# Sampling by matmuls with row weights in place of indirect gathers, in a chain of four convolution layers

## The reference, cut to what matters

```
x = x + L0(_gn(x))   # patches of 8x8 in 10x10 windows: one of 8 experts per patch (argmax of the
                     # routing logits), 3x3 convolution, bias, relu, times the softmax probability
x = x + L1(_gn(x))   # 3x3 convolution with weights mixed from 4 experts per image
x = x + L2(_gn(x))   # every pixel replaced by its nearest of 512 codes of 32 channels
x = x + L3(_gn(x))   # 3x3 deformable convolution:
    px, py = positions of 9 taps per pixel, from a 1x1 convolution of the input
    sampled = bilinear sample of the image at (px, py), zero outside
    out = 3x3 convolution, stride 3, of the sampled taps
```

## Time and profile before

| | us |
|---|---|
| median of 3 runs | 3292.12 (3291.43 to 3294.28) |
| the profiled execution | 3283.97 |
| its span, first to last instruction | 3282.1 |
| POOL busy | 2332.2 |
| PE busy | 1852.2 |
| DVE busy | 1597.8 |
| ACT busy | 710.1 |
| mean granted clock of PE, share of full | 0.711 |

### The profile page before, as it was taken

One profiled execution on the slowest core, in us unless ns is written; L12 is line 12 of the kernel. 1 busy time (PEld: TensorE's weight loads), 2 busy tenths in 40 slices (PEclk: granted clock), 3 DMA queues, 4 the chain that ended last, 5 costly groups with the idle time before them and its releaser, 6 DMA issues.

```text
span 3282.1 us, 31069 instructions
## 1 busy us (share of the span) xinstructions
PE 1852.2 (56%) x10418; PEld 1066.7 (33%) x10418; DVE 1597.8 (49%) x2862; ACT 710.1 (22%) x1865; POOL 2332.2 (71%) x2324
## 2 busy tenths in 40 slices
PE   5666775286743866367752966347862767422222
PEld 3343433153422533144331534124431534201000
DVE  3383476334753367334763357434673347522222
ACT  1141232022311323122320223112320223100000
POOL 1007777777777777777777777777777777777776
PEclk9887886588755977578765987569865788555555
DMA  4005213332135213152134222252132421211111
GB/s 81 20 25 116 69 52 89 78 76 71 52 91 106 70 51 89 54 103 69 52 90 98 64 65 69 73 104 69 52 88 57 99 70 52 83 52 54 53 52 48
DMA packets 225793, 230.24 MB, mean 70 GB/s; under 512 B 147028, under 2 KB 184324, under 8 KB 224612
## 3 DMA queue, kind: packets, MB, share of 16 engines
q0 software_dynamic: 74352, 152.18, 17.1%
q1 hardware_dynamic: 150132, 71.88, 10.8%
q10 hardware_dynamic: 1152, 4.19, 0.5%
HBM read 188.12 MB, written 39.96 MB: 69 GB/s over the span
## 4 chain that ended last, share of the span: by engine, by line
PE 32%; POOL 23%; DVE 18%; issue 10%; SPq 5%; DMA 4%; DVEq 4%; ACT 4%; POOLq 0%; ACTq 0%
POOL ring L330 23%; PE bank L824 14%; PE bank L871 5%; PE bank L857 4%; SPq L269 4%; DVE code L680 3%; DVEq L530 2%; DVE top L677 2%; PE bank L769 2%; DMA arena<-windows 2%; DVE pair L532 2%; PE bank L778 2%; PE bank L834 2%; PE bank L879 1%; PE bank L890 1%
## 5 line engine op out<-in xcount | busy, mean ns | idle before, releaser
L330 POOL DMA_INDIRECT ring<-cells,idx_sb x2304 | 2323.3, 1008 | 937.3 <-issue 697.6
L778 PE MATMUL bank<-ident_sb,samp 128*128 128x128 f32 (+1 forms) x768 | 198.8, 387 | 902.2 <-DVE samp L537 901.7
L529 DVE TENSOR_TENSOR ring<-ring,wq 128x1152 f32<-128x1152 f32 x256 | 348.0, 1359 | 692.2 <-DMA ring<-cells,idx_sb 691.4
L824 PE MATMUL bank<-arena,w 96*128 96x320 f32 x1920 | 553.4, 446 | 20.8 <-DMA arena<-windows 20.8
L824 PEld LDWEIGHTS bank<-arena,w 96*128 96x128 f32 x1920 | 369.0, 195 | 189.9 <-issue 28.0
L778 PEld LDWEIGHTS bank<-ident_sb,samp 128*128 128x128 f32 (+1 forms) x768 | 93.8, 164 | 990.5 <-DVE samp L537 961.1
L769 PE MATMUL bank<-samp_t,wc 128*32 128x128 f32 (+1 forms) x1536 | 341.5, 358 | 96.1 <-ACT samp_t L364 96.1
L622 DVE TENSOR_TENSOR ex<-ex,rtb 128x640 f32<-128x640 f32 x160 | 131.9, 824 | 452.0 <-ACT ex L388 452.0
L871 PE MATMUL bank<-cb,xs 128*128 128x512 f32 x512 | 331.7, 744 | 24.2 <-ACT xs L420 18.2
L363 ACT COPY samp_t<-bank 128x256 f32<-128x256 f32 x256 | 95.3, 372 | 995.0 <-PE bank L778 995.0
L769 PEld LDWEIGHTS bank<-samp_t,wc 128*32 128x32 f32 (+1 forms) x1536 | 158.0, 131 | 294.3 <-ACT samp_t L364 167.9
(11 more groups left out here) (122 smaller groups left out, 1365.5 us busy)
## 6 DMA issues: line engine op xcount, KB each, us to landing
ring<-cells,idx_sb POOLq DMA_INDIRECT x2304, 2.5
arena<-windows SPq DMA_DIRECT2D x96, 250.0 KB, 7.8
cells<-arena SPq DMA_DIRECT2D x32, 576.0 KB, 7.0
windows<-blocks SPq DMA_DIRECT2D x32, 312.5 KB, 4.9
y_patches<-blocks SPq DMA_DIRECT2D x32, 160.0 KB, 3.6
blocks<-y_patches SPq DMA_DIRECT2D x32, 156.2 KB
xres<-in_x ACTq DMA_DIRECT2D x8, 512.0 KB, 4.1
out<-fin SPq DMA_DIRECT2D x32, 128.0 KB, 2.0
```

Of the source, the lines that this page charges most:

```text
L330: pool.indirect_dma_start(ring[:, n % RING, CORN * C * k:CORN * C * (k + 1)], None, table[g % 2][i], bass.IndirectOffsetOnAxis(ap=idx[:, g ...
L529: dve.tensor_tensor(q, q, w.broadcast_to([128, TAPS * CORN, C]), ALU.mult)
L778: m = pe.transpose(PT[0:k, 128 * r:128 * (r + 1)], samp[:, n % 2, 128 * r:128 * r + k], ident[:])
L824: m = pe.matmul(PP[2 * (i % 2) + h][:, 0:ROWN], w0[:, dx, h, :], a, start=(dx == 0), stop=(dx == 2))
```

## The change

It touches four things.

**L3, sampling.** No indirect gathers. The image of group g lies in SBUF as `picture`: 128 partitions are 4 blocks of columns x 32 rows, and there are 2 such halves (KC), each with 5 columns x 32 channels = 160 values. The position of a tap is split into a block of four columns and a rest. One number for each pixel and tap, z, holds row and block together. PE turns z into rows (L1170), SP writes them to DRAM, and for each tile SP reads 1152 of them back into all 128 partitions (L308, `zs`, 4 buffers). ACT makes the row weights relu(1 - |z + row_at|) from them, two Abs of 1152 elements and one Relu of 2304 (L514, L517, `tent`, 3 buffers). For each tap and half, PE multiplies the tent, as 128 x 128 weights, by the picture, 160 moving columns (L1014, into three banks). DVE multiplies by the column weights `near` (L708, 480 elements from PSUM) and sums over 5 columns (L713), three times a tile. PE turns the samples (L1001), ACT copies them (L504), and once in four tiles PE convolves the four images of one pixel range, each in its own 32-partition strip (L990). A tile is now 128 pixels of image n mod 4, so that four in a row are the four images.

**L0.** For each patch POOL fetches the weights of its one expert by an indirect DMA (L476, two halves of 100 rows of 18,432 bytes), SP writes them to DRAM and reads them back in slices beside the windows (L369, L371; five slices of 13 DMAs for each group, three buffers). L1074 convolves patch by patch: 96 x 32 weights, 64 moving columns, and the four images in four 32-partition strips of the output. DVE adds the bias and then applies relu and gate (L808, L811). The relus on ACT, the gates on four experts and the summing matmuls are gone. The routing of group g+1 is computed within `front(g)`.

**L2.** The one-hot matrix is not turned. ACT writes the code numbers on a diagonal (L581), a matmul with ones spreads them over all partitions (L1122), ACT copies them (L588), and DVE compares them with each partition's own number (L891, four times 512 for each 128 pixels of four images). 48 bf16 matmuls of 128 columns then pick the codes, again in four strips (L1132), straight in the layout of the image.

**Order.** The tiles of group g-1 are spread over `front(g)` by new tables, and the last seven of each group run in the rows of L0 of the front after the next, that is, seven tiles are shifted by one front.

On PE, in the scoring stage of L2, before: one tile stands among twenty scorings (`cb,xs` are the codebook and the staged pixels).

The diff, cut to its core:

```diff
-        SLOTS = {"windows": (0, 1), "route": (1, 3), "conv1": (10, 13), "scores": (13, 14), "norm3": (16, 18),
-                 "rest": (18, GROUP_TILES)}
-        ROW_SLOTS = {0: {1: 3}, 1: {1: 4}, 2: {1: 5}, 3: {0: 6, 2: 7}, 4: {1: 8}}
-        Y_SLOT = 9
-        SCORE_SLOTS = {2: 14, 5: 15}
+        ROW_SLOTS = {0: (-7, -6), 1: (-6, -4), 2: (-4, -3), 3: (-3, -1), 4: (-1, 0)}
+        Y_SLOTS = (0, 3)
+        POOL_SLOTS = (3, 5)
+        MIX_SLOTS = (5, 7)
+        CONV1_SLOTS = (7, 9)
+        NORM2_SLOTS = (9, 11)
+        SCORE_SLOTS = {0: (11, 12), 1: (12, 13), 2: (13, 14), 3: (14, 15), 4: (15, 16), 5: (16, 17), 6: (17, 18)}
+        LAST_SLOTS = (18, 19)
+        Q_SLOTS = (19, 21)
+        NORM3_SLOTS = (21, 23)
+        REST_SLOTS = (23, GROUP_TILES - 7)
+        ALL = GROUPS * GROUP_TILES
...
+                sp.dma_start(zs[:, N % SPREADS, :],
+                             bass.AP(src.tensor, src.offset + TAPS * 128 * n, [[0, 128], [1, TAPS * 128]])
+                             ).then_inc(spread_in[N % SPREADS], 16)
...
                 for i in range(IMG):
+                    a = win_dram[i].rearrange("(p c) s -> c p s", c=C)[:, NV * v:NV * (v + 1)]
                     for dy in range(3):
+                        sp.dma_start(xs0[s][C * dy:C * (dy + 1), i], a[:, :, dy * WIN:dy * WIN + CUT]
+                                     ).then_inc(sliced[s], 16)
+                sp.dma_start(w0[s].rearrange("p n i d o -> p (n i) (d o)"),
+                             w_dram[IMG * NV * v:IMG * NV * (v + 1)].rearrange("n h (p w) -> (h p) n w", w=3 * C)
+                             ).then_inc(sliced[s], 16)
...
-                    for k in range(TAPS):
-                        pool.indirect_dma_start(
-                            ring[:, n % RING, CORN * C * k:CORN * C * (k + 1)], None, table[g % 2][i],
-                            bass.IndirectOffsetOnAxis(ap=idx[:, g % 2, i, t, k:k + 1], axis=0),
-                        ).then_inc(gathered[n % RING], 16)
...
+                pool.indirect_dma_start(picked[h if k == 0 else 0], None, A["Wexp"],
+                                        bass.IndirectOffsetOnAxis(ap=expert[:, h:h + 1], axis=0)).then_inc(w_picked[h], 16)
...
-                        act.activation(ex0[:, i, h, :], PP[2 * (i % 2) + h][:, 0:ROWN], ACT.Relu,
-                                       bias=bexp[:, h:h + 1]).then_inc(relu_done, 1)
...
-                    act.copy(onehot_t[:, i % 2, :], P2[:, :]).then_inc(turned_sb, 1)
...
+            def make_tent(N):
+                if N >= ALL:
                     return
+                act.wait_ge(spread_in[N % SPREADS], 16 * (N // SPREADS + 1))
+                if N >= TENTS:
+                    act.wait_ge(strip_done, THIRDS * (N - TENTS + 1))
+                w = tent[:, N % TENTS].rearrange("p c d n -> p c (d n)")
+                for c in range(KC):
+                    act.activation(w[:, c], zs[:, N % SPREADS, :], ACT.Abs, bias=row_at[:, c:c + 1])
+                act.drain()
+                w = tent[:, N % TENTS].rearrange("p c d n -> p (c d n)")
+                act.activation(w, w, ACT.Relu, bias=1.0, scale=-1.0).then_inc(tent_ready, 1)
...
+            def slot(N):
+                if N % SET == 1 and N > SET:
+                    copy_result(N // SET - 1)
+                if 0 < N <= ALL:
+                    copy_samples(N - 1)
+                if N % GROUP_TILES >= GROUP_TILES - IMG and N < ALL:
+                    order_picture(N // GROUP_TILES + 1, N % GROUP_TILES - GROUP_TILES + IMG)
+                make_tent(N + 2)
...
+                    for i in range(IMG):
+                        m = act.activation(diag[:, i, :], ident_h[:], ACT.Copy, scale=code_f[:, t % 2, i:i + 1])
+                    m.then_inc(diag_ready, 1)
...
+                    act.copy(spelt[:], P2[:, :]).then_inc(spelt_sb, 1)
...
-                dve.tensor_tensor(q, q, w.broadcast_to([128, TAPS * CORN, C]), ALU.mult)
-                dve.tensor_tensor(pair[:].rearrange("p k x c -> p k (x c)"), q[:, :, 0], q[:, :, 1], ALU.add
-                dve.tensor_tensor(samp[:, n % 2, :].rearrange("p (k c) -> p k c", c=C), pair[:, :, 0], pair[:, :, 1],
-                                  ALU.add).then_inc(samp_ready, 1)
...
+                for d in range(THIRDS):
+                    j = THIRDS * N + d
+                    dve.wait_ge(strip_done, j + 1)
+                    y = strip[:, j % 2].rearrange("p (d c) x -> p d c x", d=DENSE)
+                    w = near[:, b % 2, i, t, DENSE * d:DENSE * (d + 1)].unsqueeze(2)
+                    dve.tensor_tensor(y, STRIPS[j % 3][:, 0:DENSE * XW * C].rearrange("p (d c x) -> p d c x", d=DENSE, c=C),
+                                      w.broadcast_to([128, DENSE, C, XW]), ALU.mult).then_inc(strip_read, 1)
+                    if d == 0 and N >= 2:
+                        dve.wait_ge(samp_turned, N - 1)
+                    dve.drain()
+                    m = dve.tensor_reduce(samp[:, N % 2, PARTK * d:PARTK * (d + 1)], strip[:, j % 2], AX.X, ALU.add)
+                m.then_inc(samp_ready, 1)
...
+                    dve.tensor_tensor(y, PP[v % 2][:, 0:ROWN].rearrange("p (n s) -> p n s", s=PS * PS),
+                                      gb[:, 1, n].unsqueeze(2).broadcast_to(shape), ALU.add).then_inc(conv0_read, 1)
+                    dve.drain()
+                    dve.scalar_tensor_tensor(out=y, in0=y, scalar=0.0, in1=gb[:, 0, n].unsqueeze(2).broadcast_to(shape),
+                                             op0=ALU.max, op1=ALU.mult).then_inc(yc_done, 1)
...
-                        dve.tensor_scalar(onehot[:, j, :], iota[:], code[:, j, 0:1], None, ALU.is_equal
-                                          ).then_inc(onehot_ready, 1)
+                    for c in range(CCH):
+                        m = dve.tensor_scalar(onehot[:, c, :], spelt[:], code_at[:, c:c + 1], None, ALU.is_equal)
...
+                dve.scalar_tensor_tensor(out=px, in0=u, scalar=-float(BLK), in1=px, op0=ALU.mult, op1=ALU.add)
+                dve.tensor_scalar(u, u, FAR, -MIDDLE, ALU.mult, ALU.add)
+                dve.drain()
+                dve.tensor_tensor(z[:].rearrange("p t i d -> p i t d"), u, py, ALU.add).then_inc(rows_ready, 1)
...
-                            m = pe.matmul(PP[2 * (i % 2) + h][:, 0:ROWN], w0[:, dx, h, :], a,
-                                          start=(dx == 0), stop=(dx == 2))
-                            m = pe.matmul(P4[C * i:C * (i + 1), 0:ROWN], sume[:], ex0[:, i, h, :],
-                                          start=(h == 0), stop=(h == 1))
+                    for n in range(NV):
                         for dx in range(3):
+                            for i in range(IMG):
+                                a = xs0[s][:, i, n, dx:CUT]
+                                a = bass.AP(a.tensor, a.offset, [a.ap[0], [WIN, PS], [1, PS]])
+                                m = pe.matmul(PP[v % 2][C * i:C * (i + 1), PS * PS * n:PS * PS * (n + 1)],
+                                              w0[s][:, n, i, dx, :], a, start=(dx == 0), stop=(dx == 2))
+                    m.then_inc(conv0_done, 1)
...
-                    m = pe.matmul(PO[C * i:C * (i + 1), 0:128], wc[0:k, r, :], samp_t[0:k, r, :],
-                                  start=(r == 0), stop=(r == 2))
+                for r in range(3):
+                    for i in range(IMG):
+                        m = pe.matmul(PO[C * i:C * (i + 1), :], wc[:, r, :], samp_t[:, i, r, :],
+                                      start=(r == 0), stop=(r == 2))
...
-                    m = pe.transpose(PT[0:k, 128 * r:128 * (r + 1)], samp[:, n % 2, 128 * r:128 * r + k], ident[:])
+                for r in range(3):
+                    m = pe.transpose(PT[0:PARTK, 128 * r:128 * (r + 1)], samp[:, N % 2, PARTK * r:PARTK * (r + 1)],
+                                     ident[:])
...
+                for e in range(DENSE):
+                    for c in range(KC):
+                        m = pe.matmul(STRIPS[j % 3][:, XW * C * e:XW * C * (e + 1)],
+                                      tent[:, N % TENTS, c, DENSE * d + e], picture[:, b % 2, i, c],
+                                      start=(c == 0), stop=(c == KC - 1))
+                m.then_inc(strip_done, 1)
+
+            def slot(N):
+                strips(N, 0)
+                if N > 0:
+                    turn_samples(N - 1)
+                strips(N, 1)
+                strips(N, 2)
+                if N % SET == 0 and N > 0:
+                    convolve(N // SET - 1)
...
+                    pe.matmul(P2[:, :], ones_h[:], diag[:].rearrange("p i n -> p (i n)"), start=True, stop=True
...
-                            m = pe.matmul(P4[:, C * i:C * (i + 1)], onehot_t[:, i % 2, 128 * c:128 * (c + 1)],
-                                          codes_b[:, k, C * c:C * (c + 1)],
-                                          start=(c == 0 and k == 0), stop=(c == CCH - 1 and k == PARTS - 1))
+                    for c in range(CCH):
```

(5 more changed lines are left out.)

1110 lines of the change are left out of this document (632 added, 478 removed).

## The result

The changed kernel takes 2760.4 us (median of 4 runs, 2759.1 to 2768.1) against 3291.96 us (4 runs, 3291.4 to 3294.3) for the kernel before: a ratio of 0.8389 with a 95% interval of 0.8373 to 0.8405. The prediction was 2690 us, range 2330 to 3150. The profiled execution has a span of 2757.2 us at a mean granted clock of 0.911, where before had 0.711.

What follows compares the result with a forecast made beforehand. POOL's queue of gathers bounds the kernel before; without it PE, DVE and ACT set the pace. 245 + 290 + 6 x 320 + 221 = 2676 us of span, with 10 us to the median 2690 us, range 2330 to 3150.

Steps and rivals of the forecast that it cites:

- The sum: Whole kernel: first front 245, front 1 290, six steady fronts of 320 and tail 221 make a span of 2676 us.
- first front: Start of the kernel, before any tiles: weights fetched, stored and reloaded, a shorter convolution; 245 us (225 to 280).
- front 1: Second front, no tiles in its rows of L0, waits for slices at 7.8 us a landing: 290 us.
- five steady fronts: Fronts with the previous group's tiles spread over them: PE's work, stops and low clock, 320 us each.
- last front and tail: End of the kernel: a front at 320 us, then 39 tiles without a front, 221 us.
- The tile on PE: Strips 4.85 us, transposes 0.32 and convolution 0.19, with waits on semaphores 5.5 us a tile.
- the slower rival: Weight loads not hidden behind the strips' short matmuls: a tile takes 9.2 us, the kernel 3650 us; chance 5%.
- DVE and ACT: Their work for one tile: DVE 4.3 us, ACT 5.3 us, or 5.6 if each ACTIVATE costs 0.1 us more.
- The front on PE: PE's work for one group's front, L0, L1, scores and picking codes: 82 us, with 32 tiles 258 us.
- The stops: Places in a steady front where PE waits at DVE's lumps or for front results: 48 us a group.
- everything dense: Rival: the lead covers all stops and the clock stays full, 262 us a group, 2280 us; chance 12%.
- not overlapped: Rival: PE's and DVE's front work stand in turn, 385 us a group, 3120 us; chance 20%.

Runs made afterwards that it cites:

- run 8: Not a run's label: in "had itself run 8 us below its median" it is a verb, said of the profiled execution of the kernel before.
- the kernel with half of the strips: The changed kernel with only the first half of the picture multiplied, nine matmuls a tile in place of 18: 2568.2 us.
- half of the tents: The changed kernel with one Abs and one Relu of 1152 elements a tile, used for both halves, all matmuls kept: 2742.7 us.
- the kernel with pictures last: The changed kernel with SP's 16 picture loads put behind the row loads of a front's last tiles, from the second front on: 2757.1 us.

## Why the prediction was right, step by step

**The sum.** By the starts of L0 the differences are: first front 248.5 against 245, +3.5; front 1 330 against 290, +40; five steady fronts of 327.6 against 320, +38; last front and tail 540.5 against 541 (9 less than a steady front and 222 us of tail; this front prepares no next group). Together 81 us, and 2676 + 81 = 2757, the span. The median lies 3 us above it, not 10: the profiled execution of before had itself run 8 us below its median.

**The tile on PE** was the term that mattered most, and it held: 5.53 us for 5.5. What I had added for waits on semaphores, 0.14 us, isn't there: in the tail PE is busy throughout, and the 36 passes, the transposes and the convolution are each a little longer, 4.89, 0.40 and some 0.23 us for 4.85, 0.32 and 0.19. The chain (start us, us) has the 36 passes, and the tail's timeline shows the strips of a tile behind a lot of transposes:

```profile
319.96 4.89 PE bank L1014 x36
```

```profile
2602.85 0.49 PE L1001 MATMUL bank<-ident_sb,samp 128*96 128x128 f32 x3
2603.18 5.06 PE L1014 MATMUL bank<-picture,tent 128*128 128x160 f32 x36
```

4.89 us for 36 is 0.136 us a pass, forecast 0.135. (A matmul's mean of 313 ns counts its overlap with its neighbours; the spacing is what it costs.) PEld is busy 202 of PE's 210 us in the tail and costs nothing, so the slower rival falls. The rule quoted from the Trainium skill, "TensorE: Matmul & The Clock Gate", section "The mechanism", disagrees with this trace, for float32 weights of 128 columns on all rows before 160 moving columns, and the measurement decides. Where fewer columns move than are loaded, the load seems to count. L1156 has 128 columns of weights and 72 moving ones; the granted clock there is 0.50, that is 1.2 GHz:

```profile
1197.83 3.69 PE L1156 MATMUL bank<-wgrid,xn 128*128 128x72 f32 x16 [7.64 <-ACT xn L608]
1201.31 2.27 PE L1163 MATMUL bank<-ident_sb,xp 128*128 128x128 f32 x9
```

Its 16 passes start 0.218 us apart (1197.83 to 1201.31). By the tile's 0.136 us for 160, doubled for the clock, 72 moving columns would be 0.12 us; L930's 0.105 us for 128 columns, doubled, is 0.21. No run varied this. ACT at 87% of the tail fell short of the "above 90%" that I had named.

**DVE and ACT.** 0.656 and 0.653 us where 0.65 stood; 1.249, 2.124 and 0.471 us for 1.15 (1.25 with the surcharge that I had left out of the 5.3 us), 2.15 and 0.5. Even so ACT gets through a tile in 4.86 us, as the kernel with half of the strips shows: the 0.3 us of gaps in my 5.3 aren't there, since its instructions overlap by about 0.1 us (two Abs take 2.40 us, not 2.50). L514 has a bias for each partition and L517 an immediate one. With half of the tents L517 has 1152 elements for 2304 and takes 1.164 us for 2.124, so an element costs 0.83 ns, and 0.29 us of L514 and 0.20 of L517 are fixed. The Trainium skill, "ScalarE: Activation LUTs", section "What ACT_TABLE_LOAD costs", says 0.28 us for an ACTIVATE with a bias of one value a partition and 0.19 with an immediate one. The traces agree. `zs` landed in 4.2 us, forecast 4.7.

**The front on PE** was smaller than I took it, for two reasons. For L0 the bounds were 9.5 and 63 us and I chose 20 for fear of weights of its own; for the codes I took 12 of 12 to 40. The rows of one steady front, L0 from the timeline and 48 code passes from the chain:

```profile
906.08 1.86 PE L1074 MATMUL bank<-slice 96*32 96x64 f32 x120
907.87 1.90 PE L1014 MATMUL bank<-picture,tent 128*128 128x160 f32 x12
```

```profile
1111.16 0.79 PE bank L1132 x48
```

120 passes of L0 every 1.79 us, 9 us a group: four strips side by side, each pass with weights of its own, take 0.060 us for four. And 48 bf16 passes in 0.79 us are 6 us a group, 0.066 us for four where I had carried over the float32 price of 0.126. So the front is 82 - 11 - 6 = 65 us at the full clock, if the other terms held. PE's busy time in a steady front was 265.5 us, which leaves 265.5 - 177 - 65 = 23.5 us where I had 14 for the low clock. Not all of it is the clock: spreading, offsets, image and z rows (L1122, L1156, L1163, L1170), for which I had 4 us, are busy 9.9 us in the front from 906.1 us, part of them at 1.2 GHz. Together it came to less than the 176 + 82 + 14 = 272 foretold. That a steady front came out at 327.6 for 320 is partly luck: 6.5 us less work stood against 14 us more of stops.

**The stops** are 62 us for 48. By place, in the front from 906 us: feature sums 4.2 us (2 foretold); adding, normalising and pooling 8.8 (10), though the row names `feat_t`, whose copy stands behind that lump on DVE; windows and mixed weights 4.6 (5); before the scores 4.3 (4), as a wait for `fin`; flat copy 7.6 (9); z 6.3 (5). The one place that was off is the scoring: `code`, `xs`, `diag`, `onehot` and two of `fin` are 20.5 us, where I had 10. Its timeline on PE:

```profile
1108.41 1.10 PE L1115 MATMUL bank<-cb,xs 128*128 128x512 f32 x2 [1.32 <-DVE code L884]
...
1120.39 1.10 PE L1115 MATMUL bank<-cb,xs 128*128 128x512 f32 x2 [1.31 <-DVE code L884]
```

The step repeats after 11.98 us, just the 12 foretold: DVE sets it, and what PE did faster in the picking of codes turned into waiting for DVE. So seven steps have 13.4 us of stops for 8.4. The other half of the miss is the last step, whose scores, diagonal and comparison PE waits for in turn with no tile between: 7.1 us where I had 1.6. Another 3.5 us are the tent behind `zs`.

**Front 1** is the step that failed, 40 of the 81 us. I had granted it "7.8 us a landing"; PE's waits there, and what SP issues meanwhile (start us, us):

```profile
PE bank L1074 <- DMA slice<-picked_weights: 21.2, 1, 21.2
PE bank L1074 <- DMA arena<-picked_weights: 20.3, 3, 11.2
```

```profile
257.56 6.73 SPq L369 DMA_DIRECT2D arena<-windows  x12
...
264.81 8.67 SPq L319 DMA_DIRECT2D arena<-flat  x16
273.53 10.51 SPq L308 DMA_DIRECT2D zs<-z_rows  x5
284.08 5.72 SPq L369 DMA_DIRECT2D slice<-windows  x12
```

A slice is 13 issues, 6 to 7 us of SP's time ahead of a landing, and sixteen picture loads and five `zs` stand in front of the fourth slice, which PE waits 21.2 us for. With no tiles in the rows of L0, nothing covers this. The prediction named SP's order as a way to be wrong and gave it no price. The price could be had from the row of SP's issue, 0.44 us: three slices and these 21 loads are 60 issues, 26 us; they took 39, from 251.3 to 290.3. Of the 13 us more, 8 are the five `zs`: 2.1 us an issue here, where the median of all 256 is 0.32. Why they are slower here no run tells. Of the 40 us of front 1, 34 are the slices (41.5 us for the 7.8 granted); the rest is other stops, as in a steady front.

**The rivals.** The steady fronts' 327.6 us lie between "everything dense" (262 us a group) and "not overlapped" (385), somewhat nearer the latter, and so does the whole: 2760 us between 2280 and 3120.

## What to carry to other kernels

Price a matmul by the spacing inside a burst of its like, at its own type, and look twice where it moves fewer columns than it loads. Don't pad a bound that a row already shows: here strips of 32 partitions side by side cost about one pass for four. When the bound moves from a queue to compute engines, the time is the busiest engine's work plus each lump of another engine that it must wait for, and speeding up work in front of such a wait buys less than it saves: here 27 of 78 us. Count the issues on the queue that loads for the critical engine, above all in a stage where the cover is missing, since re-ordering that queue only moved the wait here.

## What the runs showed of the hardware that I had not expected

The kernel of gathers has no single time: medians of 3284 to 3299 us on some chips, and 4240 to 4251 us on two others, while a gather takes 1.0 us in every trace. (The slow chips have traces only with six and three gathers.) Yet the kernels without gathers of corners ran at 2742 to 2757 us on the two slow ones as well. There the change is worth a ratio of 0.65 (0.6489 for the kernel with pictures last). In the trace with six gathers PE, DVE and ACT stand still for 16 to 23 us at a time while POOL issues; why, no run here tells.

A plain DMA costs POOL 0.58 us to issue (1.10 us for that of the weights). SP takes 0.32 us (`zs`) or 0.44 us (slices) in the median, but up to 2.8 us for a `zs`, as in front 1.
